# Adapter matmuls of two banks moved behind the next tile's first product, the narrow product split by token block, and bias rows transposed on TensorE

## The reference, cut to what matters

```
x = x + ffn0(cond0(x))       # cond0: codebook-quantized weight plus low rank; ffn0: base + bias + routed rank-16 adapters
x = x + ffn1(cond1(x, ids))  # cond1: base + bias + the adapter that ids gives a sequence (64 tokens); ffn1: base + routed adapters

base   = x @ W.T (+ b)
logits = x @ W_router.T                                  # 8 experts, top 2, softmax weights w[t, e]
out    = base + 2 * sum_e w[t, e] * (x @ A[e].T) @ B[e].T
```

## Time and profile before

| | us |
|---|---|
| median of 3 runs | 912.09 (911.99 to 912.55) |
| the profiled execution, its own time | 914.59 |
| its span | 912.8 |
| TensorE busy in it | 904.0 (99%) |
| VectorE, ScalarE, GpSimd busy | 616.2, 312.7, 145.3 |
| HBM traffic | 191 MB, 209 GB/s over the span |

### The profile page before, as it was taken

How to read it: one execution, slowest core, us unless ns; L and a number is a source line. 1 busy time by engine, 2 the same in 40 slices (tenths; PEclk the granted TensorE clock), 3 DMA queues, 4 the chain that set the end, 5 groups by cost and what they waited for, 6 DMA issues and landing times.

```text
span 912.8 us, 13364 instructions
## 1 busy us (share of the span) xinstructions
PE 904.0 (99%) x4672; PEld 789.1 (86%) x4672; DVE 616.2 (68%) x1311; ACT 312.7 (34%) x502; POOL 145.3 (16%) x298
## 2 busy tenths in 40 slices
PE   8999999999999999999999999999999999999998
PEld 8999998888998878888888888888888788888886
DVE  6789899776587959976465566566566566566563
ACT  6579788411224424232322222222222222212220
POOL 0100010111001001414213113113113113113110
PEclk9999999999999999999999999999999999999999
DMA  8523330665612032556887887887887887887875
GB/s 338 189 95 122 119 124 24 234 210 190 141 50 93 4 135 90 212 217 226 277 277 253 285 272 259 286 270 260 286 269 261 285 267 260 290 266 263 286 226 182
DMA packets 63090, 191.51 MB, mean 210 GB/s; under 512 B 10664, under 2 KB 13100, under 8 KB 61104
## 3 DMA queue, kind: packets, MB, share of 16 engines
q1 hardware_dynamic: 52448, 159.19, 50.8%
q0 software_dynamic: 10432, 31.35, 11.4%
q10 hardware_dynamic: 144, 0.13, 0.1%
HBM read 158.93 MB, written 32.23 MB: 209 GB/s over the span
## 4 chain that ended last, share of the span: by engine, by line
PE 88%; DMA 7%; DVE 3%; ACT 1%; issue 0%; SPq 0%; DVEq 0%; ACTq 0%
PE bank L852 26%; PE bank L518 13%; PE bank L519 13%; PE bank L520 13%; DMA t_lo<-t_scratch 5%; PE bank L826 5%; PE bank L835 5%; PE bank L663 2%; PE bank L909 2%; PE bank L923 2%; PE bank L922 2%; PE bank L924 2%; PE bank L580 1%; DMA x_raw<-xq 1%; DMA m_raw<-m1t 1%; DMA w<-e_scratch 1%
## 5 line engine op out<-in xcount | busy, mean ns | idle before, releaser
L852 PE MATMUL bank<-g_hi,xs 128*128 128x512 f32 x448 | 145.2, 395 | 0.0
L852 PE MATMUL bank<-t_hi,xs 128*128 128x512 f32 x336 | 113.4, 396 | 1.6 <-DMA t_lo<-t_scratch 1.4
L489 POOL DMA_DIRECT2D p1sel<-p_scratch x128 | 65.3, 510 | 280.2 <-issue 280.2
L852 PEld LDWEIGHTS bank<-g_hi,xs 128*128 128x128 f32 x448 | 83.2, 188 | 16.5
L954 ACT ACTIVATE xs<-x_raw 128x1024 fp32r<-128x1024 f32 x60 | 62.0, 1056 | 81.3 <-PE bank L852 55.7
L852 PE MATMUL bank<-g_lo,xs 128*128 128x512 f32 x224 | 88.3, 394 | 0.0
L1277 DVE TENSOR_TENSOR xs<-x_raw,xs 128x1024 fp32r<-128x1024 f32 x60 | 75.2, 1274 | 17.2 <-ACT xs L954 16.7
L518 PE MATMUL bank<-gx,xs 128*128 128x304 f32 x256 | 77.4, 302 | 0.0
L520 PE MATMUL bank<-gx,xs 128*128 128x304 f32 x256 | 77.4, 302 | 0.0
L519 PE MATMUL bank<-gx,xs 128*128 128x304 f32 x256 | 77.3, 302 | 0.0
L852 PEld LDWEIGHTS bank<-t_hi,xs 128*128 128x128 f32 x336 | 62.0, 188 | 16.6 <-DMA t_lo<-t_scratch 4.4
(11 more groups left out here) (321 smaller groups left out, 2064.2 us busy)
## 6 DMA issues: line engine op xcount, KB each, us to landing
t_hi<-t_scratch SPq DMA_DIRECT2D x82, 512.0 KB, 4.5
t_lo<-t_scratch SPq DMA_DIRECT2D x82, 512.0 KB, 5.9
x_raw<-xq SPq DMA_DIRECT2D x16, 1024.0 KB, 6.9
out<-ost SPq DMA_DIRECT2D x64, 256.0 KB, 4.7
p1sel<-p_scratch POOLq DMA_DIRECT2D x64, 192.0 KB, 4.7
w_raw<-wall SPq DMA_DIRECT2D x16, 512.0 KB, 4.3
w<-e_scratch SPq DMA_DIRECT2D x6, 1024.0 KB, 5.1
ea<-e_scratch POOLq DMA_DIRECT2D x8, 644.0 KB, 4.2
```

What stands on the lines that cost most here:

```text
L489: pool.dma_start(f(p1sel[b][STK * s:STK * s + STK, cs]), p1_dram[bass.ds(i * STK, STK), cs]).then_inc(sems[b], 16)
L852: mm = nc.tensor.matmul(bk[j][:], l[:, c, :], m[:, c, :], start=first and c + k == 0, stop=c + k == KH + 1, skip_group_check=True)
```

## The change

It touches both parts.

- *Prologue, bias.* `bv` is transposed on TensorE into bank 7 ahead of narrow row 1, VectorE copies and splits the turned [12, 128] tile (three small instructions in step r = 1), and SyncE stores it as rows of 512 B. ScalarE waits for those stores (`st_b`) before it writes `sb_row`, whose last row lies over the tile.
- *Prologue, block 7.* Both halves of it are made before the first half of x.
- *Tiles 2 to 15.* `x_product` of the next tile is issued by token block, and `mid_terms` of bank 3 comes between the two, that of bank 0 behind the second. `mid_terms` of banks 2 and 1 come behind product 0 of the next tile. The m0 transposes move to i = 16. `m0_terms(0)` moves from `low_terms` to before product 48. A separate `u3_sum` takes what was the second use of `p5_sum`; `out_sum` of bank 3 comes before `front`, those of banks 2 and 1 at the beginning of the next tile.

```diff
-CHAIN = [(30, 44, 62, 76), (10, 24, 42, 56), (12, 28, 44, 56)]
+CHAIN = [(30, 44, 62, 76), (10, 24, 42, 56), (16, 28, 44, 56)]
...
+        u3_sum = at("u3_sum", [P, 512], F32, r2 + 55296)
...
-        bv_hl = small("bv_hl", [P, 2, 10], F32R)
+        bvt_hl = at("bvt_hl", [12, 2, P], F32R, r1 + 63488)
+        bvt = at("bvt", [12, P], F32, r1 + 64512)
@@ sync @@
-            sp.wait_ge(bias_ok, 1)
+            sp.wait_ge(bias_ok, 2)
             for k in range(2):
-                sp.dma_start(b_dram[k].rearrange("(m p) -> p m", p=P), f(bv_hl[:, k, :]),
-                             allow_slow_non_contiguous=True).then_inc(st_b, 16)
-            sp.dma_start(b_dram[2, 0:P].rearrange("(m p) -> p m", p=P), bv[:, 10:11],
-                         allow_slow_non_contiguous=True).then_inc(st_b, 16)
+                sp.dma_start(b_dram[k].rearrange("(m p) -> m p", p=P), f(bvt_hl[0:10, k, :])).then_inc(st_b, 16)
+            sp.dma_start(b_dram[2:3, 0:P], bvt[10:11, :]).then_inc(st_b, 16)
@@ tensor, prologue @@
             for r in range(KC + 1):
+                if r == 1:
+                    pe.wait_ge(bias_ok, 1)
+                    nc.tensor.transpose(bk[7][0:12, P:2 * P], bv[:], ident).then_inc(bias_mm, 1)
@@ tensor, winograd_products @@
                 product(0, 3, quarter(1, 1, 1), (t_hi, t_lo), True, lambda: t_loaded(1, 0)).then_inc(t_free, 1)
+                if n:
+                    mid_terms(tau - 1, (2, 1))
...
                 pe.wait_ge(p1_ok, n + 1)
+                m0_terms(0)
                 product(48, 0, quarter(0, 0, 1), g_quarter(1, 0), False).then_inc(p2_mm, 1)
@@ low_terms @@
-                    if j in (0, 3) or tau < REG:
+                    if j == 3 or tau < REG:
                         m0_terms(j)
@@ the loop over tiles @@
                     low_terms(tau, (3,))
-                    x_product(tau + 1)
+                    x_product(tau + 1, (0,))
+                    mid_terms(tau, (3,))
+                    x_product(tau + 1, (1,))
+                    mid_terms(tau, (0,))
                 else:
                     mid_turn(tau)
                     low_terms(tau, (0, 2, 1, 3))
-                mid_terms(tau)
+                    mid_terms(tau)
@@ scalar @@
+            act.wait_ge(st_b, 48)
             for q in range(4):
                 act.wait_ge(g_mm, MP1 + q + 1)
...
-            act.wait_ge(ld_x, 16)
-            x_hi_part(0, 0).then_inc(x_hi_s, 1)
             act.wait_ge(ld_b1, 112)
             act.wait_ge(g_mm, MP4 + 4)
             block_high(ta_hi, w1)
+            act.wait_ge(ld_x, 16)
+            x_hi_part(0, 0).then_inc(x_hi_s, 1)
...
                 if n:
-                    act.wait_ge(ev[2], tau)
+                    act.wait_ge(u3_ok, n)
@@ vector, prologue @@
-            link(nc.vector.tensor_copy(bv[:, 10:11], bk[7][:, 10:11]))
-            link(nc.vector.tensor_copy(bv_hl[:, 0, :], bv[:, 0:10]))
-            lo_of(bv_hl[:, 1, :], bv[:, 0:10], bv_hl[:, 0, :]).then_inc(bias_ok, 1)
+            nc.vector.tensor_copy(bv[:, 10:11], bk[7][:, 10:11]).then_inc(bias_ok, 1)
...
+                if r == 1:
+                    v.wait_ge(bias_mm, 2)
+                    turned = bk[7][0:12, P:2 * P]
+                    nc.vector.tensor_copy(bvt[:], turned)
+                    link(nc.vector.tensor_copy(bvt_hl[:, 0, :], turned))
+                    lo_of(bvt_hl[:, 1, :], turned, bvt_hl[:, 0, :]).then_inc(bias_ok, 1)
...
+            block_low(7, ta_lo, w1, ta_hi)
             x_low(0, 0)
-            block_low(7, ta_lo, w1, ta_hi)
             x_low(0, 1)
@@ vector, tiles @@
+                if n:
+                    v.wait_ge(u3_ok, n)
+                    out_sum(tau - 1, 3, 2, u3_sum)
+                    out_sum(tau - 1, 4, 1, u4_sum)
                 m0_low(tau)
...
                 v.wait_ge(t_free, 6 * n + 6)
-                nc.vector.tensor_tensor(p5_sum[:], bk[3][:], p5_sum[:], ALU.add).then_inc(u3_ok, 1)
+                if n:
+                    v.wait_ge(ev[2], tau)
+                nc.vector.tensor_tensor(u3_sum[:], bk[3][:], p5_sum[:], ALU.add).then_inc(u3_ok, 1)
...
                 if tau + 1 < NT2:
                     s_low(tau + 1)
-                    front(tau + 1, lambda: out_sum(tau, 1, 3, p1_sum))
+                out_sum(tau, 1, 3, p1_sum)
+                if tau + 1 < NT2:
+                    front(tau + 1)
                 else:
-                    out_sum(tau, 1, 3, p1_sum)
-                v.wait_ge(u3_ok, n + 1)
-                out_sum(tau, 3, 2, p5_sum)
-                v.wait_ge(u4_ok, n + 1)
-                out_sum(tau, 4, 1, u4_sum)
+                    v.wait_ge(u3_ok, n + 1)
+                    out_sum(tau, 3, 2, u3_sum)
+                    out_sum(tau, 4, 1, u4_sum)
```

More of the change, by code:

```diff
@@ L706, in _ @@
             block_ready(1)
-            pe.wait_ge(bias_ok, 1)
+            pe.wait_ge(bias_ok, 2)
             adapter_row(bk[7], 0, b11, True)
@@ L752, in _, with x_product @@
             vt = lambda v, b: v[:, b * P:b * P + P]
-            def x_product(tau):
+            def x_product(tau, blocks=(0, 1)):
                 u = tau if tau < REG else 0
@@ L759, in x_product @@
                 pe.wait_ge(gsel_ok, tau + 1)
-                for b in range(2):
+                for b in blocks:
                     cs, ts = slice(SX * b, SX * b + WX), slice(b * P, b * P + P)
@@ L764, in x_product @@
                                            gx[:, c, cs], gx[:, 9 + c, cs], c == 0, c == KC - 1)
-                mm.then_inc(xx_mm, 1)
+                if 1 in blocks:
+                    mm.then_inc(xx_mm, 1)
             def turn(v, n0):
@@ L912, in low_terms, with mid_terms @@
                     mm.then_inc(low_mm, 1)
-            def mid_terms(tau):
+            def mid_terms(tau, banks=(3, 0, 2, 1)):
                 pe.wait_ge(midt_hi_s, tau + 1)
@@ L918, in mid_terms @@
                     pe.wait_ge(af_lo_s, 3)
-                for j in (3, 0, 2, 1):
+                for j in banks:
                     b, h = j // 2, j % 2
```

## The result

The changed kernel takes 916.88 us (median of 5 runs, 915.65 to 918.17) against 912.09 (5 runs, 911.29 to 913.44): a ratio of 1.0050, 95% interval 1.0034 to 1.0066. It is slower by 3 to 6 us. The forecast was 913.5 with a range up to 916.0.

A forecast was written before the change was run, and what follows sets the result against it. TensorE, busy 904.0 of 912.8 us, was taken to bound the kernel. The terms -0.8 + 0.1 - 0.4 + 2.5 = +1.4 gave 916.0 for the profiled execution and 913.5 for the median, range 909.6 to 916.0 (8 in 10).

The forecast's parts named there:

- t4: Load for product 36: need and issue both shift 1.4 us, so its wait stays; -0.4 us, bounds -3.4 and +4.
- u3_ok: New wait before TensorE adds to bank 3 after product 72: 0.18 us a tile, 2.5 in all; bounds 0 and 3.5.
- Only the second half has a gain, of about 0.2: t4's load: its second half gains about 0.2 us, since it used to wait for TensorE as well.
- such a rival at 0.12: t4's load waits for ScalarE's copy, shares DMA engines with x and lands later: +4 us, 917.9; chance 0.12.
- Block 7 and the bias rows: Prologue: earlier additions remove the stall before the quarter rows, -0.8 us; the bias transpose and wait on TensorE cost +0.1.
- 2 or 3 us forecast: Prologue, SyncE's queue: the wait for the bias stores falls to 2 or 3 us, with no other trace on TensorE.
- rival 4: The bias stores' queue was holding the prologue: up to 14.5 us less, 899; chance 0.02.
- t3, t1 and the other moved waits: Tiles: t3 gets 0.7 us more time, t1 is needed 2.1 sooner; taken as 0, like the other moved waits.
- The fixed part as a sum: Terms without t4: prologue stall -0.8, bias rows +0.1 and the new wait for bank 3 +2.5.
- From one execution to the median: The sum on the profiled execution's 914.59 gave 916.0; the runs' median, 2.5 us lower, gave 913.5.
- Waits for `t_lo` as often as now: Sign in the tiles of the trace after: TensorE waits for `t_lo` as often as before the change.
- Beyond 3 us in all: Sign against the prediction: it is wrong if the wait for `t_lo` grows beyond 3 us in all.

The follow-up runs named there:

- e7: The changed kernel with t4's loads cut to a quarter of each row (part of product 36 on stale data): 912.07 us.
- e6: The kernel before with t4's loads cut to a quarter of each row (part of product 36 on stale data): 910.01 us.
- e0: The changed kernel run again, unaltered, as control on another chip: 915.84 us, ratio 1.0039 to the kernel before.
- e3: The changed kernel with SyncE issuing the load of t4 ahead of the store of bank 0: 912.01 us, ratio 1.0003 to the kernel before.
- e1: The changed kernel with m0's three matmuls for bank 0 put back in low_terms, in front of the wait for u3_ok: 913.18 us, ratio 1.0016.
- e4: The changed kernel with m0's bank 0 matmuls back in low_terms and t4 loaded ahead of the store of bank 0: 911.13 us, ratio 1.0003.
- e2: The kernel before with only the two prologue edits, block 7 ahead of x and turned bias rows: 911.97 us, ratio 0.9993.
- e12: The kernel before with x's loads cut to a quarter from the fifth tile on (later tiles on stale x): 912.37 us, ratio 1.0009.
- e13: The changed kernel with x's loads cut to a quarter from the fifth tile on (later tiles on stale x): 914.53 us, ratio 1.0028.
- e10: The kernel before with the prologue edits and the stores of banks 0, 2 and 1 behind the load of t1: 912.26 us, ratio 0.9996.
- e11: The changed kernel with u3_ok covered, t4 loaded first, and stores of banks 0, 2 and 1 behind the load of t1: 911.59 us, ratio 0.9987.
- e5: The kernel before with SyncE issuing the load of t4 ahead of the store of bank 0: 914.07 us, ratio 1.0014.
- e8: The kernel before with the prologue edits and t4 loaded ahead of the store of bank 0: 912.51 us, ratio 0.9997.
- first batch: The runs of e0, e1, e3 and e4 on one chip, with the kernel before beside them at 912.34 us.

## Why the prediction was wrong, step by step

The forecast came out 3.4 us too low. What failed is the term "I take -0.4 over all tiles" for t4: in the first set of runs it makes 3.1 of the 3.4, in the second, where +1.4 was forecast and +3.5 measured, 1.8 of the 2.1.

- **t4, forecast -0.4, measured +0.9 to +2.7.** Set by set it is what the change costs less the 2.06 without waits (e7 less e6): (916.88 - 912.09) - 2.06 = 2.7 in the first set of runs and (915.84 - 912.34) - 2.06 = 1.4 in the second. Taken from pairs that ran side by side, the waits are worth 915.84 - 912.01 = 3.8 after (e0 less e3) and 912.92 - 910.01 = 2.9 before (before less e6): 0.9 more. Against that, with `u3_ok` covered the waits are worth 2.05 (e1 less e4), no more than before. So the size is known to a microsecond at best. The traces are as coarse: over twelve tiles, what lies above the tile without waits is 2.2 (e2) and 3.2 (before), against 3.9 and 5.0 (after, e0), but 1.7 in e1. The mechanism was the one in the text: the load waits behind ScalarE's copy of bank 0. Its first issue was forecast at 3.2 and came at 3.28. "Only the second half has a gain, of about 0.2" is the sentence that failed: the first issue went from 1.84 to 3.28; the third, which TensorE had held to 2.93, came at 4.26 and gained 0.1; the fourth, the last, went from 3.29 to 4.73 and gained nothing. The need moved by as much, 1.4. The room stayed 8.0 us (7.97 before, 7.98 after), the time to landing is 7.5 (e2) and 7.7 us on average before, 7.8 in both profiles after, and up to 8.8 and 8.9. With the room in the middle of the scatter, a few tenths of landing time decide how many tiles wait: 6 of 14 before, 9 in the first profile after, 6 with longer waits in e0, 2 in e1. I had such a rival at 0.12 and priced it at 917.9.
- **What lengthens the waits at the same room isn't shown.** x's load is now 6.2 us ahead of that of t4, where it was 6.65; that is the rival's own argument, and e12 and e13 don't settle it. The store of bank 3 has moved away from the load, from 2.4 to 5.6 us ahead of it. e10 shows that moving stores behind takes 0.6 us off the landing.
- **u3_ok, forecast 0.18 a tile and 2.5 in all, measured 0.12 and 1.7** (the rows above, and e1). The place and the mechanism were right. The weight load started 0.05 behind the addition, not 0.12 as in the earlier trace rows. By the Trainium skill, page "TensorE: Matmul & The Clock Gate", step 1 of "What happens when you issue a matmul", weight loads are pulled ahead of matmuls in flight; here none was pulled ahead of the semaphore wait, the load stood until 596.18 and went at 596.23.
- **Not foreseen: 0.10 a tile, 1.3 in 13 tiles.** e1, without the new wait, still takes 34.11 where before takes 34.01. The matmuls are the same; what differs is how often the stream changes its kind. By medians over twelve tiles, the twelve `mid_terms` matmuls take 2.745 us in one stretch before and 2.773 in three (3, 3 and 6) in e1; product 0 is longer by some 0.02, product 12, which m0's transposes at i = 16 now cut in two, by some 0.02, `x_product` by 0.007. That is about 0.08 of the 0.10. That the cuts are the cause is argued from these places; no run varied them alone. I had counted a moved matmul at its old price.
- **Block 7 and the bias rows, forecast -0.8 and +0.1, measured -0.7 together** (e2, whose interval holds 0 too; its traces give 0.7 where the wait stands, and nearly nothing where it does not). In the timeline after nothing stands before the quarter rows; the addition that used to be late (first row) ends at 338.18, two microseconds ahead of the matmul that needs it (third row):

```profile
337.50 0.68 DVE L1660 TENSOR_TENSOR gl_raw<-gl_raw,bank 128x512 f32<-128x512 f32 x1
...
339.89 0.39 PE L520 MATMUL bank<-g_hi,c_lo 128*128 128x512 f32 x1
...
340.12 0.39 PE L518 MATMUL bank<-ta_hi,c_hi 128*128 128x512 f32 x1
```

The turned columns are one matmul (lines view: busy us, mean ns, idle before), and SyncE's wait of 14.5 us has become 0.8 (list of waits):

```profile
L676 PE MATMUL bank<-pk,bv 128*12 128x128 f32 x1 | 0.3, 271 | 0.0
```

```profile
SPq L371 <- DMA b_scratch<-bvt: 0.8, 1, 0.8
```

It came lower than the 2 or 3 us forecast. TensorE got nothing of the 13.7, as the sum said, and rival 4 is out. The Trainium skill, page "DMA: Bandwidth & Descriptors", section "Rules for kernel authors", has the rule against element-wise stores; the row agrees, and packets fell from 63090 to 60396, but the queue it frees was nobody's bound.
- **t3, t1 and the other moved waits, forecast 0.** Right for the change: t3 has 0 in the profiles before and after and 0.45 in e0's, t1 at most 0.06, and the list of waits after names none of the others. In the other versions t3 has up to 0.76 (e10).
- **The fixed part as a sum.** -0.8 + 0.1 + 2.5 = +1.8 forecast, 2.06 measured (e7 less e6), from +1.7 + 1.3 - 0.7 = 2.3 by its parts: nearly right by luck, because an overrated term met an omitted one.
- **From one execution to the median.** The sum was made on 914.59 and carried down 2.5 us to 912.09. The profiled execution is one of those that start at a lower clock (last section), which is worth about 1.5 of it; "at full speed throughout" is not right for it. The rest is not accounted for; tiles of one kernel vary from run to run (34.20 and 34.29 on average in e2 and before). It was no constant to carry over.

Of the marks set beforehand, the gone L518 wait, tiles of 34.2 and the load at 3.2 came true. "Waits for `t_lo` as often as now" did not: 10 weight loads against 8. "Beyond 3 us in all" was a mark on the wrong view: the list of waits held 1.4 before and after, where the runs say 2.1 to 2.9 and 3.8 to 4.8.

A better version than both is not clearly there. With the wait covered and the load ahead of the store (e4, e11) the kernel takes 911.1 to 911.6 against 912.3 to 912.9: the gain of e3's edit pays what the change costs, and 0.1% is left at most, which is what the prologue's edits alone (e2, 0.7 us) may give as well.

## What to carry to other kernels

When a transfer lands in a time that scatters around the room it has, ask for the room from its last issue to its need, at both ends, and price a shift by how many tiles cross over, not by the mean. An engine's in-order queue carries the wait of one entry to all behind it: a store that waits for another engine's copy belongs behind the loads that are due sooner, and moving work to give a load time does nothing when the same move makes the entry ahead of it late. Take the waits of the weight loads with those of the matmuls.

## What the runs showed that was not expected

- A stream of matmuls that is cut in pieces takes longer here: 0.02 to 0.03 us at each of the three places above, 0.10 a tile, with every matmul the same. Why isn't shown.
- Executions of one kernel begin in two ways, about 1.5 us apart, and the granted clock of TensorE tells them apart. In the profiles of before, e5, e8, e10, e12 and e13 it is for a stretch at half (1.2 in place of 2.4 GHz), from 10.5 to 13.9 us in before, and the sixtieth matmul starts at 18.3 to 18.7 us. In all the others it is full there, and that matmul starts at 16.8 to 17.0. Three matmuls of L580 take 0.96 us from start to start at the one and 0.52 at the other (first row before, second after):

```profile
11.71 1.17 PE L580 MATMUL bank<-m_hi,w_lo 128*128 128x388 f32 x3
```

```profile
11.18 0.69 PE L580 MATMUL bank<-m_hi,w_lo 128*128 128x388 f32 x3
```

  In both TensorE had worked with gaps of about 1 us before (0.8 and 1.0 before, 1.5 and 0.9 after); what decides between them isn't shown. It is in the times too: of the 33 executions of before in the first batch, 13 have a mean granted clock of 0.998 and a median of 913.38, the other 20 one of 911.48. The twelve times of e3 lie at 911.8 to 912.8 (nine) and at 913.4 to 913.7 (the three with 0.998). Which share a kernel draws moves its median by some tenths, and profiles of two kernels are best compared from tile to tile.
- SyncE's issue of one DMA sometimes takes 1.1 us in place of 0.43. When it hits t4, the loads behind it are that much later; in the timeline after, tile 3:

```profile
470.26 0.43 SPq L410 DMA_DIRECT2D t_hi<-t_scratch  x1
470.74 1.16 SPq L412 DMA_DIRECT2D t_lo<-t_scratch  x1
471.94 0.43 SPq L410 DMA_DIRECT2D t_hi<-t_scratch  x1
472.41 0.43 SPq L412 DMA_DIRECT2D t_lo<-t_scratch  x1
```

It happened twice to the loads of t4 in the 14 tiles after, with waits of 0.26 and 0.09, and never before.
